# Rotary attention: three slots instead of two for the split softmax weights, in a kernel of eight layers on one core

## The reference

```python
q, k, v = x_norm @ Wq.T + bq, x_norm @ Wk.T + bk, x_norm @ Wv.T + bv      # (B, S, 16 * 64)
q, k = apply_rope(split_heads(q), split_heads(k))
scores = einsum('bhqd,bhkd->bhqk', q, k) / sqrt(64)
attn = softmax(scores, axis=-1)                                           # S = 1024
out = einsum('bhqk,bhkd->bhqd', attn, v)
x = x + out.reshape(B, S, 1024) @ Wo.T + bo
```

## Time and profile before

| | before |
|---|---|
| median of 3 runs | 2794.84 us (2794.7 to 2797.34) |
| profiled execution, its own time | 2796.8 us |
| its span, first to last instruction | 2795.0 us |
| busy over the span: PE, DVE, ACT, POOL | 87%, 72%, 54%, 67% |
| granted TensorE clock, mean of the span | 0.949 of full speed |
| rotary attention's steps | from 696 to 1376 us of the span |

### The profile page before, as it was taken

How to read it: one execution, slowest core, us unless ns; L and a number is a source line. 1 busy time by engine, 2 the same in 40 slices (tenths; PEclk the granted TensorE clock), 3 DMA queues, 4 the chain that set the end, 5 groups by cost and what they waited for, 6 DMA issues and landing times. The chain is left out here.

```text
span 2795.0 us, 57341 instructions
## 1 busy us (share of the span) xinstructions
PE 2435.0 (87%) x21637; PEld 1600.0 (57%) x21822; DVE 2010.8 (72%) x3570; ACT 1520.4 (54%) x2201; POOL 1863.8 (67%) x1738
## 2 busy tenths in 40 slices
PE   6787686796899999999788999998788889999986
PEld 3455544643566666666555666666534456666655
DVE  7998455445666767767578888887386888888873
ACT  4222122323888888888625666556453256555664
POOL 1888100001899999999647899998510578999985
PEclk9998788987999999999899999999988999999999
DMA  1000000002889898889703333333211023333333
GB/s 43 1 1 1 0 23 13 4 20 65 143 147 157 147 151 154 151 149 157 131 29 56 61 62 62 61 61 69 51 30 60 16 50 65 63 61 65 62 65 62
DMA packets 632753, 193.27 MB, mean 69 GB/s; under 512 B 614920, under 2 KB 623624, under 8 KB 632480
## 3 DMA queue, kind: packets, MB, share of 16 engines
q1 hardware_dynamic: 632480, 189.60, 36.7%
HBM read 20.70 MB, written 1.05 MB: 8 GB/s over the span
## 5 line engine op out<-in xcount | busy, mean ns | idle before, releaser
L2303 PE MATMUL banks<-g_w,normed_t 128*128 128x320 f32 x1536 | 502.3, 454 | 29.4 <-DVE g_scratch L2592 29.3
L1778 DVE TENSOR_REDUCE at_negmax<-banks 128x1 f32<-128x1024 f32 x256 | 301.6, 1220 | 154.4 <-PE banks L1690 154.4
L2592 DVE TENSOR_TENSOR g_scratch<-banks,g_gate 128x640 f32<-128x640 f32 x384 | 314.3, 822 | 110.5 <-PE banks L2303 108.2
L1755 POOL TENSOR_TENSOR at_p_lo<-at_p,at_p_hi 128x640 bf16<-128x640 f32 x256 | 356.7, 1405 | 25.4 <-ACT at_p_hi L1743 22.7
L1597 DVE TENSOR_REDUCE g_negmax<-banks 128x1 f32<-128x1024 f32 x256 | 310.8, 1219 | 56.5 <-PE banks L1507 56.2
L2303 PEld LDWEIGHTS banks<-g_w,normed_t 128*128 128x128 f32 x1536 | 268.2, 193 | 123.4 <-DVE g_scratch L2592 47.0
L1561 ACT ACTIVATE g_p<-banks,g_negmax 128x1024 f32<-128x1024 f32 x256 | 285.9, 1117 | 68.9 <-DVE g_negmax L1597 61.2
L1584 POOL TENSOR_TENSOR g_p_lo<-g_p,g_p_hi 128x512 bf16<-128x512 f32 x256 | 298.2, 1186 | 30.3 <-POOL g_z L2515 18.7
L1736 ACT ACTIVATE at_p<-banks,at_negmax 128x1024 f32<-128x1024 f32 x256 | 285.7, 1116 | 6.4 <-DVE at_negmax L1778 6.4
L1574 ACT CAST g_r_hi<-banks 128x512 bf16<-128x512 f32 x128 | 75.0, 586 | 378.6 <-PE banks L1522 378.6
L1690 PE MATMUL banks<-at_k_t,at_q 64*128 64x512 f32 x1024 | 258.0, 622 | 16.5 <-POOL at_k_t L2039 8.8
(11 more groups left out here) (426 smaller groups left out, 6615.8 us busy)
## 6 DMA issues: line engine op xcount, KB each, us to landing
at_swapped<-at_crossed SPq DMA_DIRECT2D x128, 128.0 KB, 2.7
g_w<-in_ex_w SPq DMA_DIRECT2D x2, 2880.0 KB, 11.5
f_w<-in_W SPq DMA_DIRECT2D x2, 1024.0 KB, 5.7
at_rope<-in_rope SPq DMA_DIRECT2D x1, 2048.0 KB, 10.5
at_t_hi<-at_p_hi SPq DMA_TRANSPOSE x128, 3.6
at_t_lo<-at_p_lo SPq DMA_TRANSPOSE x128, 3.6
g_t_hi<-g_p_hi SPq DMA_TRANSPOSE x128, 3.1
g_t_lo<-g_p_lo SPq DMA_TRANSPOSE x128, 3.2
```

What stands on the lines that cost most here:

```text
L1755: self.nc.gpsimd.tensor_tensor(self.p_lo[:, j % 2, h, :], self.p[:, j % 2, h, 0:self.BY_DMA * P], self.p_hi[:, j % 2, h, :], ALU.subtract) ...
L1778: self.nc.vector.tensor_reduce(self.negmax[:, j % 2, h:h + 1], self.core.banks[:, first:first + 2, :], AX.XY, ALU.max, negate=True).then_i ...
L2303: nc.tensor.matmul(out[:, 0:ED], core.xt[:, at:at + P], w[:, kind * H + tile // (T * BATCH) * 2 + h, :], start=True, stop=True).then_inc(p ...
L2592: v.tensor_tensor(qk_product[:, tile % 2, kind] if kind < 2 else v_product[:, tile % 2], core.banks[:, bank:bank + 2, 0:ED].rearrange("p h ...
```

## The change

`p_hi` and `p_lo` get three slots, `j % 3`, instead of two. `act_hi` and `pool_lo` of step j therefore wait for the landing of step j-3's transfers, and no longer for that of step j-2's. `turn` reads from slot `j % 3`. The two tiles grow by 2.5 KB per partition each. `p` keeps its two slots, and no instruction is added, removed or moved.

```diff
-        self.p_hi, self.p_lo = (sb(n, [P, 2, 2, self.BY_DMA * P], BF16) for n in ("p_hi", "p_lo"))
+        self.p_hi, self.p_lo = (sb(n, [P, self.RING, 2, self.BY_DMA * P], BF16) for n in ("p_hi", "p_lo"))
...
     def act_hi(self, act, j, h):
         act.wait_ge(self.exp_done, 2 * j + h + 1)
-        if j >= 2:
-            self.wait_turned(act, j - 2)
-        self.nc.scalar.copy(self.p_hi[:, j % 2, h, :], self.p[:, j % 2, h, 0:self.BY_DMA * P]).then_inc(self.hi_ready, 1)
+        if j >= self.RING:
+            self.wait_turned(act, j - self.RING)
+        self.nc.scalar.copy(self.p_hi[:, j % self.RING, h, :], self.p[:, j % 2, h, 0:self.BY_DMA * P]).then_inc(self.hi_ready, 1)
...
     def pool_lo(self, pool, j, h):
         pool.wait_ge(self.hi_ready, 2 * j + h + 1)
-        if j >= 2:
-            self.wait_turned(pool, j - 2)
-        self.nc.gpsimd.tensor_tensor(self.p_lo[:, j % 2, h, :], self.p[:, j % 2, h, 0:self.BY_DMA * P], self.p_hi[:, j % 2, h, :],
+        if j >= self.RING:
+            self.wait_turned(pool, j - self.RING)
+        self.nc.gpsimd.tensor_tensor(self.p_lo[:, j % self.RING, h, :], self.p[:, j % 2, h, 0:self.BY_DMA * P], self.p_hi[:, j % self.RING, h, :],
                                      ALU.subtract).then_inc(self.lo_ready, 1)
...
-        sp.dma_start(dst[:, j % self.RING], src[:, j % 2].rearrange("p h n -> p (h n)"), transpose=True).then_inc(self.turned[j % self.RING], 16)
+        sp.dma_start(dst[:, j % self.RING], src[:, j % self.RING].rearrange("p h n -> p (h n)"), transpose=True).then_inc(self.turned[j % self.RING], 16)
```

## The result

The changed kernel takes 2771.16 us (median of 4 runs, 2767.76 to 2775.35) where the kernel before takes 2796.09 (four launches too, 2794.7 to 2799.44). The ratio is 0.991, with a 95% interval of 0.9892 to 0.9927: 25 us less, between 20 and 30. The profiled execution has a span of 2770.9 us, 24.1 less than the 2795.0 of before. The forecast was 2774, 21 us less. Of all the launches behind this document one is left out, of 11501.78 us, among the six of the kernel with two slots and the exchange issued last; every other lies within 0.3% of its kernel's median.

What follows compares the result with a forecast made beforehand. TensorE and GpSimd, both 96% busy, were held up by ScalarE's cast waiting for a `p_lo` transfer. Even stretch 15.8 + first unit 4.8 = 20.6, with unlisted gaps 21 us off 2794.84: 2774 us, range 2768 to 2783.

Steps and rivals of the forecast that it cites:

- The even stretch: Middle 588.7 us, 14 of the 16 units: TensorE's waits for ScalarE go, except 3.2 us; 15.8 us gained.
- The unit counted by steps: One unit of the even stretch, summed from its unstalled steps t = 0 to 7 plus 0.23 us: 40.9 us.
- The first unit: Unit without outputs to hide behind, with the worst waits: from t = 4 on 24.79 to some 20.0 us, 4.8 gained.
- steps t = 6 and 7: First unit's last steps, without projection: ScalarE's chain sets about 4.7 us each, plus 0.95 where the v split falls.
- The last unit: Third stretch, with neither exchange nor sums, steps at ScalarE's pace: no gain taken.
- GpSimd as the next bound: GpSimd's own work is 39.95 us a unit against TensorE's 40.9: it keeps up, with 0.95 us to spare.
- The rival in which it takes over: GpSimd's small gaps count in four steps of each unit, 41.8 us a unit: 8 us gained, 2787; chance 0.13.
- The slower rival: TensorE reaches the values before the transfer has landed, every engine hangs on it: 37 us lost, 2832; chance 0.04.
- the 2.6 that I gave: Margin in t = 4 between t = 2's landing at 1016.4 and TensorE's values at about 1019.0: 2.6 us.

## Why the prediction was right

- **The even stretch** was the mechanism as put: wait of the cast, late second exp, idle TensorE, late outputs' copy. The term was 15.8 us and measured 17.4: TensorE is idle for 6.4 instead of 23.8 us, and from the start of the second unit to that of the last it takes 1306.51 - 734.85 = 571.66 us, before 1332.01 - 742.94 = 589.07. (By the v splits it is 18.5, because GpSimd, behind at the start, catches up.) The 1.6 us are the gaps too short for the table of waits, 4.8 us before and 3.2 after, of which I had taken 0.4. The unit counted by steps, 40.9 us, came out at 40.8 (571.66 / 14), with one wait of 0.23 us in each.
- **The first unit**: forecast 4.8 us from t = 4 on; before 24.79, after 734.85 - 715.09 = 19.76, so 5.0. The prediction's own terms add up to 4.9 + 4.9 + 4.7 + 4.7 + 0.95 = 20.15 rather than 20.0, which would have been 4.6 gained; its steps t = 6 and 7, 10.35 us there, took 10.06.
- **What I didn't have**: the steps before t = 4 are 1.0 us shorter, 20.53 instead of 21.51 us from the first unit's second scores on. This goes with the granted clock and not with the change: from 695 to 700 us it was 0.50 before (the lower level, 1.2 GHz) and 0.74 in the mean after, and in the repeated profile of the changed kernel it was 0.50 and the steps took 21.51 us again. 17.4 + 5.0 + 1.0 = 23.4 of the 24.1 us by which the spans differ; the rest lies outside these steps. Without that 1.0 us, which is luck, the forecast of 21 is 1.4 us short. The 25 us between the medians hold 1.3 us more of that kind: with its fourth launch the kernel before moved from the 2794.84 that I counted from to 2796.09.
- **The last unit**: 37.3 us from the last v split to the last `pool_split` in both, as taken.
- **GpSimd as the next bound**: 39.95 us a unit was worked out; where GpSimd had to catch up, after the first unit, it took 39.94 (776.63 - 736.69). The DMA engines are busy for 0.91 of the stretch, as worked out. The rival in which it takes over needed its small gaps to count, and they don't: it has them where it is ahead.
- **The slower rival** named the right place, the values on TensorE, as the runs with more transfers showed. With the traffic of this kernel the margin is there: t = 2's transfer is issued at 1036.79 and needed at 1043.98, 7.2 us for the usual 3.6. The margin of 3.6 us was larger than the 2.6 that I gave, by the 1.0 us that the exchange's issues took less.
- **What the prediction missed** was not in its sum. It says that ScalarE can't cast before 1016.42 because the slot is still being read. The transfer that reads that slot had landed 5 us before, by about 1011.3; what ScalarE waited for was the other transfer, through the semaphore that both raise. It took the slot for what was scarce, and the single semaphore was. The time comes out the same either way, so the forecast could not tell the two apart; the kernel with a semaphore for each did.

The rows of TensorE and GpSimd in the changed kernel on which two of these rest:

```profile
734.85 1.99 PE L1690 MATMUL banks<-at_k_t,at_q 64*128 64x512 f32 x8 [0.45 <-ACT at_p L1736]
```

```profile
736.69 2.19 POOL L1799 TENSOR_TENSOR at_v_lo<-at_v,at_v_hi 128x1040 bf16<-128x1040 f32 x1
776.63 2.18 POOL L1799 TENSOR_TENSOR at_v_lo<-at_v,at_v_hi 128x1040 bf16<-128x1040 f32 x1
```

## What to carry to other kernels

An engine far from full (ScalarE, 86%) can be what two full ones wait for; ask of each wait what it hands on, and count TensorE's idle time, not the waiting engine's: 28.0 us on ScalarE were 17.4 us on TensorE. Before a buffer gets another slot, see whether the wait is for the transfer that reads the slot: one semaphore for two transfers makes the earlier wait for the later. An order on a queue is a balance: the exchange ahead cost a late landing, the exchange behind cost more, because it also waited for what the transfer ahead of it waited for.

## What the runs showed of the hardware

The VectorE cast from one tile to another, f32 to bf16, 128 x 1040, took 0.92 us at the least, 1.50 in the median of 15 and 7.34 at most, in the trace with that cast. The two long ones, 7.34 and 5.95 us, ran beside GpSimd instructions of 1.4 to 1.5 us that follow each other without a gap, and ended 0.56 us after GpSimd stopped. In an ordinary unit it was GpSimd that gave way a little: its pair of `pool_lo` beside the cast took 3.2 instead of 2.8 us. That the two engines can block each other over shared ports is what the Trainium skill says, "SBUF — State Buffer", section "Who interferes with whom": a VectorE cast may use both pairs of ports, of which GpSimd has one, and whoever comes first holds it for a whole instruction. That alone would cost the cast one GpSimd instruction, at most 1.5 us; here it waited past more than four. Why it was passed over is open, and that the ports are the cause is argued and not shown: no run changes them alone. Additions of VectorE that read PSUM and one tile, beside GpSimd work without a gap, showed nothing of it: 0.68 to 0.70 us in all 64.

TensorE's granted clock was 0.50, its lower level (1.2 GHz), behind 3.00 us of idle time in the kernel with four more transfers, and the same six transposes took 1.54 instead of 0.88 us.
